# Queries and keys of a fused attention and expert kernel: two float32r halves on two 64-row sides in place of three bf16 parts

## What is computed

```python
def _L0_conv_ref(x, Wq, Wk, Wv, Wproj, bproj):     # x normalised over channels; T = 1024, C = 128
    xs = jnp.reshape(x, (B, T, C))
    q = jnp.einsum('btc,hcd->bhtd', xs, Wq)         # 8 heads of size 16
    k = jnp.einsum('btc,hcd->bhtd', xs, Wk)
    v = jnp.einsum('btc,hcd->bhtd', xs, Wv)
    scores = jnp.einsum('bhtd,bhsd->bhts', q, k) * scale
    att = jax.nn.softmax(scores, axis=-1)
    out = jnp.einsum('bhts,bhsd->bhtd', att, v)
    ...
    out = out @ Wproj + bproj

x = x + _L0_conv_ref(_ln_c(x), ...)
t = _to_tokens(x)
t = t + _L0_ffn_ref(_ln_t(t), w_gating, w1, w2)     # top-2 gating over 16 experts, capacity 256, two products and a relu
x = _from_tokens(t, x)
```

## Time and profile before

| | |
|---|---|
| time, median of 3 runs | 2675.8 us (2669.5 to 2680.6) |
| span of the profiled execution | 2676.3 us |
| its first score matmul | 83.89 us |
| TensorE busy | 2423.1 us, 91% |
| VectorE busy | 1997.1 us, 75% |
| ScalarE busy | 1511.7 us, 56% |
| GpSimd busy | 1187.5 us, 44% |

### The profile page before, as it was taken

How to read it: one execution, slowest core, us unless ns; L and a number is a source line. 1 busy time by engine, 2 the same in 40 slices (tenths; PEclk the granted TensorE clock), 3 DMA queues, 4 the chain that set the end, 5 groups by cost and what they waited for, 6 DMA issues and landing times. The chain is left out here.

```text
span 2676.3 us, 67960 instructions
## 1 busy us (share of the span) xinstructions
PE 2423.1 (91%) x18706; PEld 1203.4 (45%) x18706; DVE 1997.1 (75%) x4671; ACT 1511.7 (56%) x2881; POOL 1187.5 (44%) x1833
## 2 busy tenths in 40 slices
PE   3999999999999999999999999999928999999963
PEld 1333333333333333333333333333318999999962
DVE  6888888978888888888888898889624555555544
ACT  0576666766667666666666676667703444444420
POOL 4304536363544536263543637354264444444430
PEclk9999999999999999999999999999959999999985
DMA  2233222223232222223222222322062222222249
GB/s 44 33 52 55 51 42 59 34 58 53 57 59 48 59 34 58 41 58 65 53 51 42 58 34 58 63 47 57 10 179 62 63 63 63 63 64 63 63 117 286
DMA packets 142625, 168.55 MB, mean 63 GB/s; under 512 B 25214, under 2 KB 97284, under 8 KB 142370
## 3 DMA queue, kind: packets, MB, share of 16 engines
q1 hardware_dynamic: 125474, 131.08, 23.4%
q0 software_dynamic: 16896, 34.12, 4.5%
HBM read 60.66 MB, written 44.67 MB: 39 GB/s over the span
## 5 line engine op out<-in xcount | busy, mean ns | idle before, releaser
L843 DVE TENSOR_REDUCE sb_m_red<-banks 128x1 f32<-128x512 f32 x2048 | 1363.4, 684 | 252.4 <-PE banks L1265 240.1
L706 ACT ACTIVATE sb_arena_a<-banks 128x512 f32<-128x512 f32 x2048 | 1140.7, 596 | 581.3 <-PE banks L1287 570.0
L1265 PE MATMUL banks<-sb_arena_b 96*128 96x512 bf16 x2048 | 797.7, 394 | 54.4 <-issue 32.5
L1287 PE MATMUL banks<-sb_arena_b 104*128 104x512 bf16 x2048 | 661.1, 385 | 0.9 <-DMA sb_arena_b<-sb_m_row 0.9
L1306 PE MATMUL banks<-sb_arena_a,sb_arena_d 128*32 128x256 f32 x8192 | 661.5, 395 | 0.4 <-ACT sb_arena_a L706 0.4
L1265 PEld LDWEIGHTS banks<-sb_arena_b 96*128 96x128 bf16 x2048 | 199.1, 97 | 551.5 <-DVE sb_m_red L843 310.8
L689 POOL DMA_INDIRECT expert_out<-sb_arena_d x272 | 267.4, 983 | 306.3 <-DVE sb_arena_d L1169 265.3
L1306 PEld LDWEIGHTS banks<-sb_arena_a,sb_arena_d 128*32 128x32 f32 x8192 | 162.4, 108 | 438.6 <-issue 368.8
L1444 PE MATMUL banks<-sb_arena_d,sb_arena_c 128*128 128x128 f32 x2176 | 291.1, 277 | 40.6 <-ACT sb_arena_d L814 40.6
L634 POOL DMA_INDIRECT sorted_rows<-sb_rows,sb_place x256 | 248.0, 969 | 97.1 <-issue 90.1
L1453 PE MATMUL banks<-sb_arena_c 128*128 128x128 f32 x2176 | 287.4, 276 | 0.0
(11 more groups left out here) (145 smaller groups left out, 1817.1 us busy)
## 6 DMA issues: line engine op xcount, KB each, us to landing
sb_arena_b<-sb_arena_c SPq DMA_DIRECT2D x384, 128.0 KB, 5.4
sb_arena_d<-sorted_rows SPq DMA_DIRECT2D x272, 66.0 KB, 1.8
sb_arena_a<-expert_out SPq DMA_DIRECT2D x32, 512.0 KB, 5.6
sb_x_in<-in_x_dram SPq DMA_DIRECT2D x16, 512.0 KB, 3.3
sb_res<-in_x_dram SPq DMA_DIRECT2D x16, 512.0 KB, 7.9
sb_x_all<-sb_res SPq DMA_DIRECT2D x16, 512.0 KB, 3.0
out_dram<-sb_arena_a SPq DMA_DIRECT2D x16, 512.0 KB, 3.7
expert_out<-sb_arena_d POOLq DMA_INDIRECT x272, 2.2
```

Source lines behind the costliest of these rows:

```text
L706: nc.scalar.activation(probs[:, u % PRING, :], ps_score[:, u % RING, :], ACT.Exp, scale=SCALE).then_inc(exp_done, 1)
L843: nc.vector.tensor_reduce(out=m_red[:, s % 2, u:u + 1], in_=ps_max[:, m % SLOTS % RING, :], axis=AX.X, op=ALU.max).then_inc(max_taken, 1)
L1265: nc.tensor.matmul(ps_max[:, m % SLOTS % RING, :], qs[0:STACK, g, h, half * HALF + t * P:half * HALF + (t + 1) * P], ks[0:STACK, g, h, kh ...
L1287: nc.tensor.matmul(ps_score[:, u % RING, :], ks[0:STACK + MROWS, g, h, i * P:(i + 1) * P], qs[0:STACK + MROWS, g, h, half * HALF:(half + 1 ...
```

## The change

Each query and key is now two float32r halves, rounded on the write, and three products are stacked: 3 x 16 = 48 rows, and 50 with two parts of the maximum. Heads of even number stand on rows 0 to 63 and heads of odd number on rows 64 to 127, so that a group's four heads are two layers of two sides. Its core:

```diff
-Q_PART = (0, 0, 1, 1, 0, 2)
-K_PART = (0, 1, 0, 1, 2, 0)
+Q_PART = (0, 0, 1)
+K_PART = (0, 1, 0)
 STACK = 16 * len(Q_PART)
 MPARTS = 2
+SIDES = 2
+LAYERS = HG // SIDES
+SIDE = P // SIDES
...
-        arena_b = sb("arena_b", [P, 2 * G * HG * T], BF16)
-        stacks = arena_b[:, :].rearrange("p (o g h t) -> p o g h t", o=2, g=G, h=HG)
+        arena_b = sb("arena_b", [P, 2 * G * LAYERS * T], F32R)
+        stacks = arena_b[:, :].rearrange("p (o g l t) -> p o g l t", o=2, g=G, l=LAYERS)
...
                     for r, level in enumerate(part):
-                        sp.dma_start(stacks[16 * r:16 * r + 16, o, g, :, :],
-                                     parts[64 * g:64 * g + 64, o, level, :]).then_inc(stacked[g], 16)
+                        for s in range(SIDES):
+                            to, of = SIDE * s + 16 * r, 64 * g + 32 * s
+                            sp.dma_start(stacks_f[to:to + 16, o, g, :, :],
+                                         parts[of:of + 32, o, level, :]).then_inc(stacked[g], 16)
...
-                sp.dma_start(qs[STACK:STACK + MROWS, g, :, half * HALF:(half + 1) * HALF],
-                             m_row[STACK:STACK + MROWS, :].unsqueeze(1).to_broadcast([MROWS, HG, HALF])).then_inc(
-                    m_loaded, 16)
+                for side in range(SIDES):
+                    to = SIDE * side + STACK
+                    sp.dma_start(stacks_f[to:to + MPARTS, 0, g, :, half * HALF:(half + 1) * HALF],
+                                 m_row[MPARTS * LAYERS * side:MPARTS * LAYERS * (side + 1), :]).then_inc(m_loaded, 16)
...
+            sp.dma_start(w2_dram.rearrange("e (c p) d -> (e c) (p d)", p=P),
+                         w2.rearrange("e (c p) d -> (e c) (p d)", p=P)).then_inc(w2_copied_out, 16)
+            sp.wait_ge(key_rows, KEY_ROWS)
             stack(0, 0)
...
-                nc.gpsimd.tensor_scalar(parts[:, o, 0, cols], f, 1.0, 0.0, ALU.mult, ALU.add).then_inc(qk_parts, 1)
-                for level in (1, 2):
-                    wait_apart(gp, gp_passed, qk_parts, done + 2 * level - 1)
-                    nc.gpsimd.tensor_tensor(out=f, in0=f, in1=parts[:, o, level - 1, cols],
-                                            op=ALU.subtract).then_inc(qk_parts, 1)
-                    wait_apart(gp, gp_passed, qk_parts, done + 2 * level)
-                    nc.gpsimd.tensor_scalar(parts[:, o, level, cols], f, 1.0, 0.0,
-                                            ALU.mult, ALU.add).then_inc(qk_parts, 1)
+                nc.gpsimd.tensor_scalar(parts_r[:, o, 0, cols], parts[:, o, 1, cols], 1.0, 0.0, ALU.mult,
+                                        ALU.add).then_inc(qk_parts, 1)
+                wait_apart(gp, gp_passed, qk_parts, 8 * b + 2 * i + 1)
+                nc.gpsimd.tensor_tensor(out=parts_r[:, o, 1, cols], in0=parts[:, o, 1, cols],
+                                        in1=parts[:, o, 0, cols], op=ALU.subtract).then_inc(qk_parts, 1)
...
-                h, t, kh = u // 8, u // 2 % 4, u % 2
+                side, kh, t, l = u % SIDES, u // SIDES % 2, u // (2 * SIDES) % 4, u // (8 * SIDES)
+                rows_of = slice(SIDE * side, SIDE * side + STACK)
...
-                nc.tensor.matmul(ps_max[:, m % SLOTS % RING, :], qs[0:STACK, g, h, half * HALF + t * P:half * HALF + (t + 1) * P],
-                                 ks[0:STACK, g, h, kh * HALF:(kh + 1) * HALF], start=True,
+                nc.tensor.matmul(ps_max[:, m % SLOTS % RING, :],
+                                 qs[rows_of, g, l, half * HALF + t * P:half * HALF + (t + 1) * P],
+                                 ks[rows_of, g, l, kh * HALF:(kh + 1) * HALF], start=True,
...
-                    last = nc.tensor.matmul(misc[STACK:STACK + MROWS, t * P:(t + 1) * P],
-                                            m_parts[:, t, :, :].rearrange("p a h -> p (a h)"), ident_b[:, :],
-                                            start=True, stop=True)
+                    last = nc.tensor.transpose(misc[0:MROWS, t * P:(t + 1) * P],
+                                               m_parts_f[:, t, :, :, :].rearrange("p s a l -> p (s a l)"), ident[:, :])
...
+                l, side = h // SIDES, h % SIDES
+                rows_of = slice(SIDE * side, SIDE * side + STACK + MPARTS)
...
-                nc.tensor.matmul(ps_score[:, u % RING, :], ks[0:STACK + MROWS, g, h, i * P:(i + 1) * P],
-                                 qs[0:STACK + MROWS, g, h, half * HALF:(half + 1) * HALF], start=True,
+                nc.tensor.matmul(ps_score[:, u % RING, :], ks[rows_of, g, l, i * P:(i + 1) * P],
+                                 qs[rows_of, g, l, half * HALF:(half + 1) * HALF], start=True,
```

More of the change, by code:

```diff
@@ L6 @@
 FP32 = mybir.dt.float32
+F32R = mybir.dt.float32r
 BF16 = mybir.dt.bfloat16
@@ L102, in metaformer @@
         expert_out = nc.dram_tensor("expert_out", (2 * B * T, C), FP32, kind="Internal").ap()
+        w2_dram = nc.dram_tensor("w2_dram", (E, HID, C), FP32, kind="Internal").ap()
         table_dram = nc.dram_tensor("table_dram", (2, 3 * P), I32, kind="Internal").ap()
@@ L715, in copy_qk @@
             def copy_qk(b, i):
+                o, half = i // 2, i % 2
                 wait(act, qk_psum, 4 * b + i + 1)
-                wait(act, qk_parts, 20 * b + 5 * (i - 1))
-                nc.scalar.activation(qk_f[:, i % 2, :], misc[:, :], ACT.Copy).then_inc(qk_copied, 1)
+                if i == 0:
+                    for g in range(G):
+                        wait(act, stacked[g], STACKED * b)
+                nc.scalar.activation(parts[:, o, 1, half * HALF:(half + 1) * HALF], misc[:, :],
+                                     ACT.Copy).then_inc(qk_copied, 1)
             def copy_v(b, half):
@@ L841, in take_max @@
                 s, u = m // UNITS, m % UNITS
+                side, kh, tl = u % SIDES, u // SIDES % 2, u // (2 * SIDES)
+                at = (tl * SIDES + side) * 2 + kh
                 wait(dve, max_ready, SLOTS * b + m + 1)
-                nc.vector.tensor_reduce(out=m_red[:, s % 2, u:u + 1], in_=ps_max[:, m % SLOTS % RING, :], axis=AX.X,
+                nc.vector.tensor_reduce(out=m_red[:, s % 2, at:at + 1], in_=ps_max[:, m % SLOTS % RING, :], axis=AX.X,
                                         op=ALU.max).then_inc(max_taken, 1)
@@ L848, in row_maxima @@
                 wait(dve, max_taken, UNITS * (k + 1))
-                wait(dve, m_split, 3 * (k - 1))
+                wait(dve, m_split, 2 * (k - 1))
                 nc.vector.tensor_reduce(out=m_neg[:, s % 2, :],
@@ L856, in split_m @@
                 k = STAGES * b + s
-                neg = m_neg[:, s % 2, :].rearrange("p (t h) -> p t h", t=HG)
-                rest = m_rest[:, :].rearrange("p (t h) -> p t h", t=HG)
-                wait(dve, m_split, 3 * k + step)
+                neg = m_neg[:, s % 2, :].rearrange("p (l t s) -> p t s l", l=LAYERS, t=HG)
+                wait(dve, m_split, 2 * k + step)
                 if step == 0:
@@ L1023, in _ @@
             for o in range(2):
-                nc.vector.tensor_copy(wq_r[:, o, :].rearrange("c (g d h) -> c g d h", g=G, d=D),
-                                      wq_in[:, o].rearrange("c (g h) d -> c g d h", g=G)).then_inc(setup_v, 1)
+                for g in range(G):
+                    nc.vector.tensor_copy(
+                        wq_r[:, o, 64 * g:64 * g + 64].rearrange("c (s d l) -> c s d l", s=SIDES, d=D),
+                        wq_in[:, o, HG * g:HG * g + HG, :].rearrange("c (l s) d -> c s d l", s=SIDES)).then_inc(
+                        setup_v, 1)
             dve.wait_ge(wg_mean, 1)
@@ L1037, in _ @@
                 cols = slice(half * HALF, (half + 1) * HALF)
[L1038 removed]
                 dve.wait_ge(qk_copied, i + 1)
[L1040 to L1046 removed]
+                nc.vector.tensor_copy(parts_r[:, o, 0, cols], parts[:, o, 1, cols]).then_inc(qk_parts, 1)
+                dve.wait_ge(qk_parts, 2 * i + 1)
+                nc.vector.tensor_tensor(out=parts_r[:, o, 1, cols], in0=parts[:, o, 1, cols], in1=parts[:, o, 0, cols],
+                                        op=ALU.subtract).then_inc(qk_parts, 1)
             for m in range(LEAD):
@@ L1060, in batch @@
                         row_maxima(b, m // UNITS - 1)
-                    if 0 < m % UNITS < 4 and not (last and m > SLOTS + 4):
+                    if 0 < m % UNITS < 3 and not (last and m > SLOTS + 4):
                         split_m(b, m // UNITS - 1, m % UNITS - 1)
```

83 lines of the change are left out of this document (30 added, 53 removed).

## The result

The changed kernel takes **2847.9 us** (median of 4 runs, 2836.7 to 2880.3), the kernel before 2678.1 (median of 4, 2669.5 to 2680.6). The ratio is 1.063, 95% interval 1.058 to 1.067: slower, where 2630 us and faster than before was forecast. The ratios and intervals in this document leave out executions more than 1.5% above the fastest of the same kernel, while the medians and ranges keep them. The profiled execution is the longest of the four (2880.3 us by its own time, span 2878.6); its granted clock is 0.870, that of the other three 0.877 to 0.886.

A forecast was written before the change was run, and what follows sets the result against it. TensorE was taken as the bound. Per batch -3.3 (TensorE) + 1.2 (maxima) + 0.8 (VectorE) - 0.6 (stack) = -1.9, times 16 is -30; with -16 at the start, 2676.3 became 2630 us, range 2550 to 2785.

The forecast's parts named there:

- At the start of each batch ... the clock stands at half; nothing in the change touches this: Batch loop's start: granted clock 0.50 there, taken as unaffected by the change; no term in the sum.
- Three steps in place of four: Attention pairs: only the two scores overlap, leaving three 0.215 us steps; 0.208 us saved per pair, 10.4 us per batch.
- A float32r matmul streams like bf16: Maximum and score matmuls: 512 float32r columns taken at 0.215 us, between bounds of 0.215 and 0.43.
- Half pace: Rival, maximum and score matmuls: float32r columns take 0.43 us, +44 us per batch, near 3300 us; chance 0.09.
- The load, 59 ns, taken between 15 and 108: Exposed float32r weight load on TensorE: 59 ns, which is 44 ns above bf16's wherever it is exposed.
- full load: Rival, exposed weight loads: 108 ns, 49 ns more at 76 places, +3.7 us per batch before give-back; 2674 us; chance 0.18.
- Changes of shape: TensorE around other work: each change between 64 and 128 rows drains for 0.094 us; projections between scores 0.33 longer.
- Free changes: Rival, TensorE: no drain between 64 and 128 rows, load as for bf16; 2563 us; chance 0.12.
- TensorE's balance at full clock: TensorE in attention: 10.4 us gained less 7.1 of drains and loads, -3.3 us per batch.
- The maxima and the stack: Stage handovers: later maxima cost +1.2 us per batch at two stages; the next batch's stack wait drops, -0.6.
- The start: Before attention: shorter split and free GpSimd bring the first maximum from 55.77 to 40 us, -16 us.
- No overlap, slower (2764): Rival, each pair's two scores: different row sides do not start together, +6.5 us per batch, 2764 us; chance 0.18.

The follow-up runs named there:

- the padded kernel: Changed kernel with maxima on 62 and scores on 64 rows of each side, zeros in the added query rows: 2723.0 us.
- the kernel on all rows: Changed kernel with both heads' maximum and score matmuls on all 128 rows, those of side 1 zeros, odd heads' own scores left out: 2799.1 us.
- bf16 halves: Changed kernel with bf16 in place of float32r halves, same products and sides, fewer bits kept: 2624.6 us.
- the one-sided kernel: Changed kernel with the odd heads' matmuls also on rows 0 to 63, their own scores left out: 3859.7 us.

## Why the prediction was wrong

Taken by its own steps:

- **What bounds the kernel.** Right: TensorE's row sets the time, before and after.
- **"At the start of each batch ... the clock stands at half; nothing in the change touches this"** is the step that failed, and the whole miss lies in it: +235 us in the profiled execution, against a sum of -46. I read 0.50 in the earlier trace rows as a fixed toll of the batch start, and took the rest of the attention at full clock as before. Neither held. Behind the same standstill the clock stays at half for 3.4 to 6.8 us on 96 and 104 rows and for 20 to 27 on 48 and 50, and it now falls in places where it did not, behind the logits and behind a short wait; those places hold more of the half clock (341 us) than the turns (242). The runs: on 128, 80, 64 and 50 rows without overlap the attention's clock in the profiled executions was 0.99, 0.96, 0.78 and 0.62 (the first and last float32r, the others bf16), on 96 and 104 it was 0.98. The profiled executions on 64 and 50 rows are longer than the fastest runs, but the fastest runs, by their clock over the whole span, fall off in the same way: 0.962, 0.948, 0.861 and 0.733, and 0.966 on 96 and 104 rows. I had a rival for every price of an instruction and none for the clock. The Trainium skill, TensorE: Matmul & The Clock Gate, Part 1, says that the gate goes by how busy TensorE has been. By busy time alone this case would have kept its clock, since TensorE is busy in 97% of the attention both times; the rows count as well, as the padded kernel shows.
- **Three steps in place of four.** The overlap is there, and larger than forecast: pairs with both overlaps have two streaming steps (1.24), not three. The count of 50 was also two short, since slots 37 and 101 have neither `weigh` nor other work behind them, as slot 69. Besides the start it is the only part of the sum that was too low in gain.
- **A float32r matmul streams like bf16.** Nearly right: 0.23 between matmuls with all rows, for 0.215 to 0.22. The 14 ns were not in the sum. *Half pace* is out.
- **The load, 59 ns, taken between 15 and 108.** Mis-sized: 0.34 less 0.23 is 0.11 us where the load shows, the upper end. The place was right: in the kernel on all rows it shows once per pair, as the load of the first matmul behind `weigh`. Against bf16 halves it costs 8.1 us per batch, where 49 + 44 ns at 76 places give 7.1; the longer steps are the likely rest. The rival *full load* had its mechanism right, and its time (2674) wrong with the rest.
- **Changes of shape.** A projection between two scores:

```profile
1172.81 0.40 PE L1290 MATMUL banks<-sb_arena_b 50*128 50x512 f32 x1
1173.14 1.12 PE L1246 MATMUL banks<-sb_xt,sb_wq_r 128*128 128x512 f32 x2
1174.19 0.49 PE L1290 MATMUL banks<-sb_arena_b 50*128 50x512 f32 x1
1174.53 0.39 PE L1266 MATMUL banks<-sb_arena_b 48*128 48x512 f32 x1
```

It is 0.33 from the score to the projection, 1.05 to the next score and 0.34 from there to the maximum, for 0.22, 0.86 and 0.22 before. That is +0.42 where +0.33 was forecast, and the larger load is most of the difference. *Free changes* is out as well. From maximum to `weigh` it is 0.33 for 0.31. The drains alone weren't taken apart.
- **TensorE's balance at full clock.** -1.0 us per batch measured, -3.3 forecast for TensorE alone and -1.9 with what hangs on it. The sign was right: more overlap, dearer loads.
- **The maxima and the stack.** The copy at 1109.17 is followed by both DMAs, issued from 1109.83 in 1.26, so the second issue is about 0.6, for the 0.5 assumed. About half of the +1.2 per batch arrived. This is the first score of a stage without other work ahead of it:

```profile
1188.47 0.50 PE L1266 MATMUL banks<-sb_arena_b 48*128 48x512 f32 x1
1188.87 0.60 PE L1290 MATMUL banks<-sb_arena_b 50*128 50x512 f32 x2
1189.31 0.39 PE L1266 MATMUL banks<-sb_arena_b 48*128 48x512 f32 x1
```

From the first maximum to the second it is 0.84, where the pairs above take 0.57 and 0.35; at both such stages of a batch it is 0.79 to 0.91 whenever the clock is full, so about 0.3 is lost at each. The last packets of the maxima's DMA land at 1188.75 and the score's load starts 0.114 us behind them, here as at both such stages of nearly every batch, while the exponential that it needs was done 1.2 us before. The groups by line put only 1.8 us down to that DMA; the rest of these waits stands there under ScalarE.
- **The start.** First maximum at 37.2 for 40 forecast, -18.6 us for -16. The parts were indeed the hold; the copy was not.
- **No overlap, slower (2764).** With *half pace* (near 3300) it is a rival on the side where the result fell, both for reasons that aren't there. The range ended at 2785, 63 us short.

ScalarE's moved wait does not show as a loss anywhere in the accounting above; SyncE's second issue shows at the two stages just named.

Open: what makes the clock fall, since the standstills, the waits and the short matmuls ahead of its falls were not varied by a run; how much of the half clock that is left at 62 and 64 rows comes from waits and how much from rows, and why float32r on 50 rows loses more clock (0.86 in the attention) than bf16 on the same rows (0.92), when on 62 and 64 rows both have 0.94.

## What to carry to other kernels

Before putting matmuls on fewer rows, look at where the granted clock already dips: those dips got longer here when the matmuls behind them used fewer rows (61 us became 242), and new ones opened behind short matmuls and short waits (341 us). What they took back was many times what was gained. If rows are left over, let the matmuls run over them with zeros, which costs no time on TensorE and gave 125 us here. And cost a float32r weight load at 0.11 us for the first matmul behind a stop or a change of shape.

## What the runs showed of the hardware

- **The clock follows the rows.** Attention at 0.62 on 50 rows, 0.78 on 64, 0.96 on 80, 0.98 on 96 and 104, with TensorE busy in 97% to nearly 100% of each; and 0.86 against 0.94 for 50 and 64 rows on each of two sides. Rows that hold zeros count. In the changed kernel the falls come in the wake of a standstill (3.1 us at 1115.30), of short matmuls (128x16, at 1156.85) or of a short wait (0.88 us at 807.58).
- **A matmul on other rows starts ahead of its turn.** In program order each pair is maximum (even), score (even), score (odd), maximum (odd). In the one-sided kernel the first score is never less than 232 ns behind the maximum (354 pairs at full clock). In the changed kernel some score starts within 200 ns of it in 475 of 822, 309 of them within 50, as at 1105.71. On the maximum's own rows no run shows that, so it is taken to be the odd one; the trace doesn't name the side, so this is inferred. That is where pairs of 1.24 come from, two steps each of a maximum beside a score. The Trainium skill, TensorE: Matmul & The Clock Gate, Part 3, says that matmuls start and end in program order; if that held here, a pair would have three steps.
- **Float32r streams 512 columns in 0.23 us at full clock**, about 0.014 more than bf16, and its weight load shows 0.11 us behind `weigh` where bf16's does not.
